# A four-layer convolution and scan kernel on one core: the channel means of the first layer are summed inside the sampling stage, the mixing stage reads its input in chunks, and the gate stage of the third layer is written as a deeper pipeline

## The reference, cut to what matters

```python
# layer 0
xr = conv1x1(x, w_reduce, b_reduce)                      # 192 -> 180 channels
offs = conv1x1(xr, w_offset, b_offset)
off_w, off_h = (offs[:, :cm], offs[:, cm:])
f_w = deform_conv2d(xr, off_w, w_dcnw, b_dcnw)
f_h = deform_conv2d(xr, off_h, w_dcnh, b_dcnh)
f_avg = (f_w + f_h).mean(axis=(2, 3), keepdims=True)     # mean over all pixels
attn = jax.nn.softmax(conv1x1(f_avg, w_attn, b_attn), axis=1)
f_dcm = attn[:, 0:1] * f_h + attn[:, 1:2] * f_w
return conv1x1(f_dcm, w_expand, b_expand)

# layer 2, after the forward and backward recurrences
x_bi = 0.5 * (x_fwd + x_bwd)
h = jax.nn.sigmoid(r) * x_bi
mu = jnp.mean(h, axis=-1, keepdims=True)
var = jnp.var(h, axis=-1, keepdims=True)
h = (h - mu) * jax.lax.rsqrt(var + LN_EPS) * ln_g + ln_b
out = jnp.einsum('btc,dc->btd', h, Wo)
```

## Time and profile before

| what | us |
|---|---|
| median of three runs | 14534.5 |
| the profiled execution, device time | 14526.16 |
| its span in the trace | 14524.4 |
| sampling stage | about 8391 |
| mixing stage | about 481 |
| gate stage | about 624 |
| PE busy over the span | 13173.8 (91%) |
| ACT busy | 11848.2 (82%) |
| DVE busy | 11475.4 (79%) |
| POOL busy | 7260.6 (50%) |

### The profile page before, as it was taken

The page is one execution under the profiler, slowest core; times in us unless marked ns, Lnnn a source line. Parts: engine busy times, 40 slices in busy tenths (PEclk is TensorE's granted clock), DMA queues, the critical chain, the costliest instruction groups (busy, mean ns, idle before and its releaser), DMA issues. The chain is left out here.

```text
span 14524.4 us, 244913 instructions
## 1 busy us (share of the span) xinstructions
PE 13173.8 (91%) x80556; PEld 10401.7 (72%) x80556; DVE 11475.4 (79%) x14230; ACT 11848.2 (82%) x17113; POOL 7260.6 (50%) x3802
## 2 busy tenths in 40 slices
PE   7899999999999999999999997667077989999999
PEld 3699999999999999999999997223022335555555
DVE  4588887788878887877888786578966988888888
ACT  2599999999999999999999996119644879999998
POOL 0155555555555555555555554053310018888887
PEclk9999999999999999999999998568587889999999
DMA  4466666666666666666666667434332443333333
GB/s 107 123 171 169 171 170 169 171 171 171 170 170 172 170 171 169 172 168 170 170 171 171 170 171 161 105 87 154 122 104 76 154 138 103 102 102 102 102 102 90
DMA packets 825516, 2100.02 MB, mean 145 GB/s; under 512 B 82811, under 2 KB 439473, under 8 KB 681009
## 3 DMA queue, kind: packets, MB, share of 16 engines
q1 hardware_dynamic: 814289, 2070.18, 54.4%
q10 hardware_dynamic: 9984, 14.16, 0.3%
HBM read 1815.36 MB, written 268.74 MB: 143 GB/s over the span
## 5 line engine op out<-in xcount | busy, mean ns | idle before, releaser
L524 PE MATMUL dc_p<-dc_t 96*128 96x144 f32 x51912 | 6892.8, 286 | 30.0 <-PEq L521 29.5
L584 POOL TENSOR_TENSOR dc_t<-dc_t 128x648 f32<-128x648 f32 x2884 | 4614.4, 1600 | 4374.0 <-POOLq L583 4374.0
L524 PEld LDWEIGHTS dc_p<-dc_t 96*128 96x128 f32 x51912 | 6522.6, 189 | 75.8 <-issue 53.7
L625 DVE TENSOR_TENSOR dc_t<-dc_p,dc_t 128x1296 f32<-128x1296 f32 x2884 | 4343.7, 1506 | 987.3 <-DVEq L623 971.7
L463 ACT ACTIVATE dc_t<-dc_t 96x1152 f32<-96x1152 f32 x2886 | 3595.7, 1246 | 113.7 <-ACTq L462 111.6
L465 ACT ACTIVATE dc_t<-dc_t 96x1152 f32<-96x1152 f32 x2886 | 3360.3, 1164 | 365.1 <-ACTq L464 16.0
L1985 DVE TENSOR_TENSOR_SCAN ms_t<-ms_t,ms_p 128x512 f32<-128x512 f32 x1728 | 2128.0, 1271 | 283.0 <-PE ms_p L1927 203.5
L1901 POOL TENSOR_TENSOR ms_t<-ms_t 128x1536 f32<-128x1536 f32 x576 | 1988.0, 3457 | 503.2 <-DVE ms_t L1985 499.3
L640 DVE TENSOR_TENSOR dc_t<-dc_t 128x324 f32<-128x324 f32 x2883 | 1427.6, 495 | 684.4 <-DVEq L638 645.8
L1937 PE MATMUL ms_p<-ms_t,top_t 128*128 128x512 f32 x3456 | 1775.0, 596 | 0.0
L561 PE MATMUL dc_p<-dc_t 128*128 128x180 f32 (+1 forms) x7488 | 1655.4, 321 | 68.4 <-PEq L556 49.7
(11 more groups left out here) (206 smaller groups left out, 10090.1 us busy)
## 6 DMA issues: line engine op xcount, KB each, us to landing
dc_t<-sxd SPq DMA_DIRECT2D x1443, 864.0 KB, 5.8
ms_t<-bcd SPq DMA_DIRECT2D x576, 256.0 KB, 3.3
dc_t<-xrT SPq DMA_DIRECT2D x145, 675.0 KB, 5.7
kvd<-wk_t SPq DMA_DIRECT2D x18, 1536.0 KB, 5.1
xvd<-mi_t SPq DMA_DIRECT2D x36, 768.0 KB, 3.5
szd<-mi_t SPq DMA_DIRECT2D x36, 768.0 KB, 5.7
dld<-mi_t SPq DMA_DIRECT2D x36, 768.0 KB, 3.4
ms_t<-dld SPq DMA_DIRECT2D x36, 768.0 KB, 6.8
```

The lines of the kernel that those rows point to most:

```text
L524: ins = e.matmul(PT[j % 2][:, t // 3, (t % 3) * 144:(t % 3 + 1) * 144], HX[:, m % NHX, t * 128:(t + 1) * 128], XW[:, i, ky:ky + WIN, g * C ...
L584: e.tensor_tensor(z[:, :, 0:HALF], z[:, :, 0:HALF], z[:, :, HALF:2 * HALF], ALU.add)\
L625: e.tensor_tensor(Zt[:, n % 4, :].rearrange("p (b m i) -> p b m i", b=3, i=CG), PT[n % 2][:, :, 0:432].rearrange("p b (m i) -> p b m i", i ...
```

## The change

Three phases change.

1. Sampling: a persistent tile `SUM` [128, 2, 2, 180] is zeroed at the start, and `add_up` first adds the finished PSUM tile to it, by one more `tensor_tensor` ahead of the existing instruction.
2. Mixing: the sums over whole quarters go away. PE folds `SUM` over its 128 partitions by eight one-column matmuls, and the attention chain runs once for both images. `fd` is no longer loaded whole: both images form one stream of 48 chunks with a ring of six slots for `fd` and `x`, three for G0 and G1, three PSUM buffers and four output slots. The semaphores count upwards and are reset in a block of their own at the end.
3. Gate: the 36 chunks go through a pipeline that is up to four chunks deep, DVE's order is scale, gate, put, centre, statistics; root and reciprocal become `exp(-0.5 ln(var + eps))` on ACT, with the epsilon as its bias, so DVE loses two instructions in each chunk. Rings: nine slots for the input, four for the recurrences, five for HH, three for HN and RS.

```diff
@@ sampling, DVE
+                e.memset(k.SUM[:, :, :, :], 0.0)
...
-                def add_up(i, conv):
+                def add_up(b, i, conv):
                     e.wait_ge(s_f, 1).then_inc(s_f, -1)
+                    total = k.SUM[:, b, conv, :]
+                    e.tensor_tensor(total, total, PF[:, conv * CM:(conv + 1) * CM], ALU.add)
                     a = ACC[:, i, conv, :]
                     e.scalar_tensor_tensor(out=a, in0=a, scalar=TAB[:, i % 2, WIN:WIN + 1],
...
@@ mixing, SP
-                e.wait_ge(s_w, 96).then_inc(s_w, -96)
-                for s in s_wr:
-                    e.sem_inc(s, 1)
-                for b in range(B):
-                    if b:
-                        e.wait_ge(s_fbf, 1).then_inc(s_fbf, -1)
-                    for i in range(4):
-                        r0 = 1 + b * NT + i * QR
-                        e.dma_start(FB[:, i * QR:(i + 1) * QR, :, :],
...
+                def load(c):
+                    b, r, q = c // NCH, c % NCH, c % RF
+                    r0 = 1 + b * NT + 3 * r
+                    if c >= RF:
+                        e.wait_ge(s_g1, c - RF + 1)
+                        e.wait_ge(s_xo, 2 * (c - RF + 1))
+                    e.dma_start(FB[:, q, :, :, :], k.d["fd"][r0:r0 + 3].rearrange("y c (h p) x -> p y (c h) x", p=HM))\
+                        .then_inc(s_fb[q], 16)
+                    e.dma_start(XI[:, q, :, :], k.x_v[b, :, :, r * NP:(r + 1) * NP].rearrange("h p n -> p h n"))\
+                        .then_inc(s_xi[q], 16)
...
@@ mixing, PE and DVE
+                        ins = e.matmul(PL[:, 4 * b + i:4 * b + i + 1], k.SUM[:, b, i // 2, i % 2 * HM:(i % 2 + 1) * HM],
+                                       O1[:, :], start=True, stop=True)
...
-                        e.tensor_reduce(SM[:, i, :],
-                                        FB[:, i * QR:(i + 1) * QR, :, :].rearrange("p y c x -> p c y x"),
-                                        AX.XY, ALU.add).then_inc(s_v, 1)
...
+                for c in range(N + 2):
+                    if c >= 2:
+                        expand(c - 2)
+                    if c < N:
+                        mix(c)
+                    if c >= 2:
+                        statistics(c - 2)
...
@@ gate, SP
+                def load(n): ...
+                    if n >= RY:
+                        e.wait_ge(s_h, n - RY + 1)
...
+                for i in range(N + 6):
+                    if i + 3 < N:
+                        load(i + 3)
+                    n = i - 6
+                    if n >= 0: ...
+                        e.wait_ge(s_bn, n + 1)
...
@@ gate, ACT
+                def spread(n):
+                    e.wait_ge(s_var, n + 1)
+                    if n >= 3:
+                        e.wait_ge(s_hn, n - 2)
+                    e.activation(RS[:, n % 3, :], PV[n % 2][:, :], ACT.Ln, bias=EP[:, 0:1]).then_inc(s_ln, 1)
+                    e.wait_ge(s_ln, n + 1)
+                    e.activation(RS[:, n % 3, :], RS[:, n % 3, :], ACT.Exp, scale=-0.5).then_inc(s_rs, 1)
...
+                for i in range(N + 4):
+                    if i + 1 < N:
+                        norm(i + 1)
+                    if i < N:
+                        sigmoid(i)
+                    if 3 <= i < N + 3:
+                        affine(i - 3)
+                    if 1 <= i <= N:
+                        square(i - 1)
+                    if 2 <= i < N + 2:
+                        e.preload_act_table_set("natural_log_exp_and_others")
+                        spread(i - 2)
...
@@ gate, PE: PR(i), PO(i-4), PM(i-1), PV(i-2) in each turn i
...
@@ gate, DVE
+                for i in range(N + 4):
+                    if 3 <= i < N + 3:
+                        scale(i - 3)
+                    if i < N:
+                        gate(i)
+                    if 4 <= i:
+                        put(i - 4)
+                    if 1 <= i <= N:
+                        centre(i - 1)
+                    if 4 <= i:
+                        statistics(i - 4)
```

More of the change, by code:

```diff
@@ L697, in mix_and_expand @@
         ON = p.sb([1, HM])
[L698 to L703, removed]
-        PL = p.ps([HM, 512])
[L705 to L719, removed]
+        O1 = p.sb([128, 1])
+        MN = p.sb([HM, B, 4])
+        FA = p.sb([HM, B, 2])
+        L = p.sb([1, B, 2])
+        LM = p.sb([1, B])
+        AT = p.sb([HM, B, 2])
+        BB = p.sb([HM, B, 2])
+        PL = p.ps([HM, 512])
+        PE = [p.ps([HC, 2, 512]) for _ in range(3)]
+        (s_w, s_o1, s_mean, s_v, s_fa, s_l, s_lx, s_ex, s_at, s_ab, s_bb, s_g0, s_g1, s_pe, s_xo, s_bn) = p.sems(16)
+        s_fb = p.sems(RF)
+        s_xi = p.sems(RF)
+        s_st = p.sems(RO)
         with p.block() as blk:
@@ L746, in _ @@
+                for c in range(N):
+                    load(c)
             @blk.scalar
             def _(e):
[L748 to L766, removed]
+                e.wait_ge(s_lx, 1)
+                e.activation(L[:, :, :], L[:, :, :], ACT.Exp).then_inc(s_ex, 1)
+                e.wait_ge(s_bb, 1)
+                def store(c):
+                    b, r, q = c // NCH, c % NCH, c % RO
+                    e.wait_ge(s_bn, c + 1)
+                    e.dma_start(k.d["x1"][b, :, :, r * NP:(r + 1) * NP].rearrange("h p n -> p h n"), XO[:, q, :, :])\
+                        .then_inc(s_st[q], 16)
@@ new lines, in _ @@
+                for c in range(N):
+                    b, q = c // NCH, c % RG
+                    e.wait_ge(s_fb[c % RF], 16 * (c // RF + 1))
+                    if c >= RG:
+                        e.wait_ge(s_g1, c - RG + 1)
+                    for h in range(2):
+                        ins = e.activation(G0[:, q, h, :].rearrange("p (y x) -> p y x", x=128), FB[:, c % RF, :, h, :],
+                                           ACT.Identity, bias=BB[:, b, h:h + 1], scale=AT[:, b, 1:2])
+                    ins.then_inc(s_g0, 1)
+                    if c >= 3:
+                        store(c - 3)
@@ L768, in _ @@
+                for c in range(N - 3, N):
+                    store(c)
+                for q in range(RO):
+                    e.wait_ge(s_st[q], 16 * (N // RO))
             @blk.tensor
             def _(e):
-                e.wait_ge(s_wr[1], 1).then_inc(s_wr[1], -1)
+                e.wait_ge(s_o1, 1)
                 for b in range(B):
-                    e.wait_ge(s_fa, 1).then_inc(s_fa, -1)
-                    for h in range(2):
[L774 to L786, removed]
@@ new lines, in _ @@
+                ins.then_inc(s_l, 1)
+                e.wait_ge(s_at, 1)
+                e.matmul(PL[:, 16:20], ON[:, :], L[:, :, :], start=True, stop=True).then_inc(s_ab, 1)
+                for c in range(N):
+                    q = c % 3
+                    e.wait_ge(s_g1, c + 1)
+                    if c >= 3:
+                        e.wait_ge(s_xo, 2 * (c - 2))
+                    for m in range(2):
+                        for h in range(2):
+                            ins = e.matmul(PE[q][:, m, 0:NP], WE[:, h, m * HC:(m + 1) * HC], G1[:, c % RG, h, :],
+                                           start=(h == 0), stop=(h == 1))
+                    ins.then_inc(s_pe, 1)
@@ L1362, in _ @@
[L1362 removed]
+                        e.dma_start(Y_[:, n % RY, :, :], src[b, :, :, u0:u0 + T].rearrange("h p n -> p h n"))\
+                            .then_inc(s_yy[n % RY], 16)
+                for n in range(3):
                     load(n)
[L1364 to L1370 removed]
@@ new lines, in spread, with affine @@
+                def spread(n):
[5 more added lines that the diff above has]
+                    e.activation(RS[:, n % 3, :], RS[:, n % 3, :], ACT.Exp, scale=-0.5).then_inc(s_rs, 1)
+                def affine(n):
+                    e.wait_ge(s_hn, n + 1)
+                    for h in range(2):
+                        ins = e.activation(HN[:, n % 3, h, :], HN[:, n % 3, h, :], ACT.Identity,
+                                           bias=GB[:, h, 1:2], scale=GB[:, h, 0:1])
+                    ins.then_inc(s_af, 1)
@@ L1424, in _ @@
[L1424 to L1437 removed]
+                    return ins
```

381 lines of the change are left out of this document (192 added, 189 removed).

## The result

| | us | against before |
|---|---|---|
| before, median of 4 runs | 14534.2 | |
| changed kernel, median of 4 runs | 14183.4 (14179.6 to 14202.4) | 0.976, 95% interval 0.9743 to 0.9777 |
| predicted | 14249, range 14160 to 14325 | 0.980 |

What follows compares the result with a forecast made beforehand. It took sampling as bound by a DVE-POOL ring, mixing by the fd load, then PE, and gate by an ACT-DVE ring: 14526.2 + 89 - 205 - 170 = 14240, with 8.3 to the median 14249 us, range 14160 to 14325.

Steps and rivals of the forecast that it cites:

- Sampling, +89: Sampling: 288 added DVE additions ahead of add_up, each paid at add_up's step of 0.31 us, 89 us more.
- one ring: Sampling: halve waits for sum_rows, behind quarter, which waits for the previous halve; DVE work between quarter and sum_rows paid in full.
- Nothing is free: Sampling: no free time in the 2.80 us of a plain step, so the added DVE addition is paid.
- The addition is hidden: Rival, sampling: DVE's slack takes the addition, so the first term is 0: 14160 us, chance 0.10.
- the stall multiplies: Rival, sampling: PE waits for add_up too, and PE's and ACT's backlog adds a second equal loss: 14338 us, chance 0.08.
- Mixing, -205: Mixing: first matmul at 9004.1, then 48 chunks of 5.27 us, end at 9266 against 9471.3: 205 us less.
- PE and DMA nearly equal: Mixing: per chunk, PE's bound 5.27 us at the low clock and DMA's 5.06 us; 5.27 was taken.
- Gate, -170: Gate stage: 35 periods of 11.6 us plus start and end, finishing at 10979 against 11148.9: 170 us less.
- The sum of the ring: Gate stage: instructions and hand-overs through ACT and DVE in the new order add up to 11.2 us a period.
- for added waits: Gate stage: some 0.4 us put on the 11.2 us period, giving 11.6.
- POOL meets scale and not the product: Gate stage: POOL's addition falls on scale, off the ring; rival, it holds the gate product: 14303 us, chance 0.14.
- no drain: Gate stage: a table load costs 1.28 us without drain; rival, each switch also drains 1.38 us: 14348 us, chance 0.03.

Runs made afterwards that it cites:

- the seven executions: Seven profiled executions whose sampling code is that of the changed kernel: sampling took 8468 to 8485 us, mean 8476.
- s_both_late: Changed kernel with both instructions of add_up (addition to the sums and the existing one) moved behind sum_rows: 14200.0 us, 0.9774 of the kernel before.
- s_total_later: Changed kernel with the addition to the sums taken from SBUF, two steps after add_up and behind sum_rows: 14113.9 us, 0.9709 of the kernel before.
- g_no_pool: Changed kernel with POOL's additions in the gate stage left out: 14161.3 us (one run), gate stage 429.0 us, sigmoids 11.08 us apart.
- s_total_acc: Changed kernel with the sums taken from add_up's SBUF tile, after a wait for its end that releases the PSUM bank: 14197.6 us, 0.9769 of before.

## Why the prediction was right, and where it was off

- *Bounds by stage*: right. Each stage changed on the path that the timeline had shown. The 66 us are four misses that all point the same way: 18 in sampling, 10 in mixing, 28 in the gate stage, and 7 to 8 in the last step, where I added before's 8.3 us between profile and median, of which the changed kernel shows 0.8.
- *Sampling, +89*: the mechanism was right, the size not. I took `add_up`'s step of 0.31; the addition's is 0.25, hence 71 us. As the seven executions show, one such profile is good to some 9 us. What I called one ring is two ways, and both bear: s_both_late shows the second, s_total_later that nothing else does. "Nothing is free" was right for this place only: two steps later the same addition costs 10 us or less in all. "The addition is hidden" and "the stall multiplies" did not come.
- *Mixing, -205*: 10 us too little. The chain took 11.7 us from the first issue (I had 13.7), a chunk 5.13 instead of 5.27 (the record's modelled end was in my 10.53), the reset block some 2 of the 3 us. PE at the low clock decided, as said. "PE and DMA nearly equal" was wrong: DMA's bound is 4.41, not 5.06. I had read 114.5% as saturation at 169 GB/s, but at 109% the same 16 engines moved 260 GB/s. What limited the load of `fd` before to 169 stays open.
- *Gate, -170*: the mis-sized term, 28 us too little. The sum of the ring, 11.2, was right to 0.13 us; the 0.4 us "for added waits" did not exist (0.52 x 35 = 18 us), and the first three distances between sigmoids were 4.85, 5.89 and 9.93 while the pipeline filled, 12.6 us less than three periods. The end, from the last gate product to the next phase, took 35.7 us, 4 more than my 20 + 5 + 3.4 + 3. The 5 us for PE's cold start had no row behind them; in the end itself, the last projection ran at a clock of 0.52, its eight records taking 7.00 us where the one before took 3.67.
- *Rivals*: POOL meets scale and not the product, as argued (the product's median is 1.22 us), and g_no_pool shows that scale is off the ring. The stage is at clock 0.97. Square ends at 10586.77, the table starts at 10586.78 and the logarithm at 10588.08: no drain, so the price that the Trainium skill's page "ScalarE: Activation LUTs" gives in "What ACT_TABLE_LOAD costs" beyond the load itself is not paid in this stage either.

## What to carry to other kernels

Add up the ring that a stage runs in, instruction by instruction with the steps between starts, and give nothing for waits that no row shows; then list every engine that waits for the place where a new instruction goes, since moving it off one way helps only if it leaves the others too. Ask what bounds the stage next before the edit: here it was PE at 10.3 us a chunk in the gate stage and DMA at 4.4 in mixing, and both capped the gain.

## What the runs showed of the hardware

- Matmuls on 90 rows and 96 columns stayed at 1.2 GHz for 246 us without a gap; with zero rows added to 96 the mean clock was 0.83, to 128 it was 0.99, and mixing got 33 to 34 us shorter. Between 96 and 128 only the zero rows differ; between 90 and 96 also the memsets ahead.
- A wait of DVE for its own last instruction, with the release behind it, cost 0.44 us more than the plain sequence (0.75 in s_total_acc against 0.31 before, to the next start).
- A DMA share over 100% does not say that DMA is full: 114.5% went with 169 GB/s, 109% with 260 and 108% with 270.
- An exponential and a logarithm ran behind one load of a table (L1445, 1.28 us), and no time stood between the square, the load and the logarithm (10586.77, 10586.78 to 10588.06, 10588.08).
